# Layer 0 attention of a two-layer block: scores made once with queries on partitions, probabilities transposed on the array

## The reference

```python
h = _layernorm(x, axis=-1) * (1 + ca) + sa
q = (h @ Wq.T).reshape(B, S, 16, 64).transpose(0, 2, 1, 3)      # B = 2, S = 1024
k, v = ...                                                      # 4 heads each, repeated 4 times
scores = jnp.einsum('bhqd,bhkd->bhqk', q, k) * 64 ** -0.5
scores = scores + causal                                        # -inf above the diagonal
probs = jax.nn.softmax(scores, axis=-1)
out = jnp.einsum('bhqk,bhkd->bhqd', probs, v)
x = x + ga * (out.transpose(0, 2, 1, 3).reshape(B, S, 1024) @ Wo.T)
```

## Time and profile before

| | us |
|---|---|
| median of 3 runs | 1540.2 |
| lowest, highest | 1532.3, 1541.4 |
| span of the profiled execution | 1535.8 |
| layer 0 attention in it, first projection to last addition to y | 38.8 to 673.2 |
| one group of it in the steady part (215 to 525 us holds four) | 77.5 |

### The profile page before, as it was taken

How to read it: one execution, slowest core, us unless ns; L and a number is a source line. 1 busy time by engine, 2 the same in 40 slices (tenths; PEclk the granted TensorE clock), 3 DMA queues, 4 the chain that set the end, 5 groups by cost and what they waited for, 6 DMA issues and landing times. The chain is left out here.

```text
span 1535.8 us, 21410 instructions
## 1 busy us (share of the span) xinstructions
PE 1313.7 (86%) x7772; PEld 774.5 (50%) x7772; DVE 976.1 (64%) x1750; ACT 692.4 (45%) x1319; POOL 115.2 (7%) x155
## 2 busy tenths in 40 slices
PE   4688999999999999966999996526898888789998
PEld 3344444454545454444888874413343333256886
DVE  4455464545555454146999985756777666257998
ACT  2232334342424252433666665421566556525664
POOL 0000000000000000000000000120211111020000
PEclk9698999999999999987999998855899989868998
DMA  3101111120201020104576640022222210102220
GB/s 103 40 15 34 29 34 34 33 48 15 48 19 43 15 43 15 30 0 96 130 159 146 150 92 1 1 35 90 56 55 57 47 47 20 43 21 78 76 103 28
DMA packets 51476, 81.61 MB, mean 53 GB/s; under 512 B 16749, under 2 KB 34453, under 8 KB 47445
## 3 DMA queue, kind: packets, MB, share of 16 engines
q1 hardware_dynamic: 51004, 79.40, 21.1%
q10 hardware_dynamic: 384, 1.05, 0.6%
HBM read 63.75 MB, written 5.68 MB: 45 GB/s over the span
## 5 line engine op out<-in xcount | busy, mean ns | idle before, releaser
L621 DVE TENSOR_REDUCE mraw<-ps 128x1 f32<-128x512 f32 (+3 forms) x304 | 192.7, 659 | 131.1 <-PE ps L507 74.0
L1329 PE MATMUL ps<-qA 128*128 128x512 f32 x960 | 252.9, 400 | 15.2 <-POOL qA L1439 10.6
L723 ACT ACTIVATE shared<-ps 128x512 f32<-128x512 f32 (+1 forms) x216 | 119.4, 567 | 263.3 <-PE ps L540 261.9
L1046 DVE TENSOR_REDUCE mraw<-ps 128x2 f32<-128x1024 f32 (+3 forms) x160 | 173.7, 1114 | 67.6 <-PE ps L954 46.1
L1329 PEld LDWEIGHTS ps<-qA 128*128 128x128 f32 x960 | 182.1, 192 | 64.2 <-POOL qA L1439 12.3
L1101 ACT ACTIVATE shared<-ps 128x512 f32<-128x512 f32 (+2 forms) x320 | 154.4, 561 | 124.7 <-PE ps L970 124.4
L539 PE MATMUL ps<-qA,kH 128*128 128x512 f32 (+3 forms) x384 | 167.8, 447 | 5.8 <-DMA qB<-mT 5.8
L501 PE MATMUL ps<-kH,qA 128*128 128x512 f32 (+3 forms) x384 | 138.8, 415 | 34.9 <-DVE qA L611 18.8
L1393 ACT CAST qA<-shared 128x512 fp32r<-128x512 f32 x160 | 99.3, 621 | 90.4 <-DVE shared L1531 88.9
L1341 PE MATMUL ps<-qA,kH 128*128 128x512 f32 x480 | 136.3, 393 | 4.1 <-DVE qA L1455 4.1
L540 PE MATMUL ps<-qB,kL 65*128 65x512 f32 (+3 forms) x384 | 132.8, 356 | 0.0
(11 more groups left out here) (247 smaller groups left out, 1747.1 us busy)
## 6 DMA issues: line engine op xcount, KB each, us to landing
shared<-comb SPq DMA_DIRECT2D x92, 256.0 KB, 4.3
qB<-qA SPq DMA_DIRECT2D x16, 512.0 KB, 4.8
rB<-a0rec_dram SPq DMA_DIRECT2D x60, 128.0 KB, 2.9
shared<-comb SPq DMA_DIRECT2D x7, 1024.0 KB, 4.4
rB<-a1rec_dram SPq DMA_DIRECT2D x28, 128.0 KB, 2.6
e0wUp<-in_w SPq DMA_DIRECT2D x48, 64.0 KB, 4.6
qA<-q_split SPq DMA_DIRECT2D x24, 128.0 KB
q_split<-qA SPq DMA_DIRECT2D x4, 512.0 KB
```

What stands on the lines that cost most here:

```text
L621: nc.vector.tensor_reduce(out[:, h0:h0 + n_h, qt % 4], src, AX, ALU.max).then_inc(w_free, 1)
L723: nc.scalar.activation(probs(n)[:, hs[0]:hs[-1] + 1, lo:512], src, ACT.Exp, scale=scale)\
L1046: nc.vector.tensor_reduce(out[:, :, js[0]:js[-1] + 1, qt % 4], src, AX, ALU.max).then_inc(x_free, 1)
L1329: ins = nc.tensor.matmul(bank[0:M, :], w[par][:, at:at + M], h[:, cols], start=(r == 0), stop=(r == 2))
```

## The change

The attention of layer 0 is written anew; the other stages stay as they are.

- Scores are made once, with queries on partitions. A row m is one tile of 128 queries (qt) of one group, against its qt + 1 blocks of keys; the tiles are taken in the order 3, 4, 2, 5, 1, 6, 0, 7. A row is cut into units: all four heads at once for qt 0 and 1, two heads for 2 and 3, one head for 4 to 7. That is 22 units to a group.
- For each head and PSUM bank there is a "high" matmul (128 rows) and a "low" one (64 rows, `qA[0:64]` against `kL[0:64]`), and a mask matmul on the diagonal.
- `high` and `low` scale the queries by -0.125, so scores are negative. DVE takes the least of each row of a unit (`least_of`), ACT the exponential with that as bias and with the row's sum as a second result (`exps`), one instruction to a head.
- The probabilities are turned back, 128 x 128 at a time, by transposes on the array (`turn`): 144 to a group, four to a PSUM bank. ACT and DVE copy the banks out (`copy_turned`), 4 of 7 by ACT.
- Values are float32 matmuls with 64 columns of V as weights, two heads of 128 queries moving, two such side by side (columns 0 to 63 and 64 to 127 of the array). There are no matmuls with ones.
- One over the sums (`recip`, DVE, 128 x 4) is widened by POOL, turned by two transposes (`spread_rows`), copied by ACT, and multiplied in by DVE (`normalise`).
- The DMAs of the copy of q, of the maxima, of the sums and of their inverses are gone, with the triangle on POOL. `qB` and `rB` serve as room for turned probabilities; the constant `sel64` and the ones row of `kL` are gone.
- Projections, `fin` and turned probabilities share two banks (4 and 5), in the order of one plan; the scores have two slots of two banks, so unit s waits for the exponentials of unit s - 2.

```diff
-            (k.sel64[:, :, :], a["sel64"]), (k.dec[:, :], a["dec"]), (k.rope[:, :, :, :], a["rope"]),
+            (k.dec[:, :], a["dec"]), (k.rope[:, :, :, :], a["rope"]),
...
+    ORDER = (3, 4, 2, 5, 1, 6, 0, 7)
+    U = 1 + REP // 2
     LAG = 2
+    SLOTS = 2
+    P_RING = 4
+    PT_RING = 3
+    def heads_of(qt):
+        size = REP if qt < 2 else 2 if qt < 4 else 1
         return [tuple(range(h, h + size)) for h in range(0, REP, size)]
...
+    ROWS_OF = [(g, qt) for g in range(G) for qt in ORDER]
+    UNITS = [(m, hs) for m, (g, qt) in enumerate(ROWS_OF) for hs in heads_of(qt)]
+    NU, NM = len(UNITS), len(ROWS_OF)
...
+    def planned():
+        out = [("proj", 0, 0, j) for j in range(U)]
+        products = []
+        ready_jobs = {}
+        for g in range(G):
+            for i, (qc, j) in enumerate([(qc, j) for qc in range(2) for j in range(U)]):
+                if g:
+                    ready_jobs.setdefault(PER_GROUP * (g - 1) + 3 + 3 * i, []).append(("proj", g, qc, j))
+                elif qc:
+                    ready_jobs.setdefault(0, []).append(("proj", g, qc, j))
...
+            for m in [m for m in range(NM) if final_unit[m] + LAG == s]:
+                out.append(("recip", m))
+            blocks = []
+            for m in range(NM):
+                if first_unit[m] + LAG <= s <= final_unit[m] + LAG:
+                    blocks += [(m, b) for b in range(ROWS_OF[m][1] + 1) if closing_unit(m, b) + LAG == s]
+            credit = min(credit + 1.75, 3.0) if s < NU else 99.0
+            while products and products[0][-1] <= s and \
+                    (credit >= 1 or any(m - PT_RING >= products[0][1] for m, b in blocks)):
+                item = products.pop(0)
+                out.append(item[:-1])
+                credit -= 1
+                m = item[1]
...
+            turns = [("t", m, b, i) for m, b in blocks for i in range(4)]
+            out += woven(matmuls_of(s) if s < NU else [], turns)
+            for m in [m for m in range(NM) if final_unit[m] + LAG == s]:
+                out.append(("spread", m))
+                products += [("values", m, kt, s + 2) for kt in range(ROWS_OF[m][1] + 1)]
+            if s < NU:
+                out.append(("unit", s))
+            s += 1
+        return out
...
+                def score(e):
+                    kind, u, at, what, h = e
+                    m, hs = UNITS[u]
+                    g, qt = ROWS_OF[m]
+                    par = g % 2
+                    heads, lo, hi = banks_of(qt, hs)[at]
+                    opens = at == 0 and what == "high" and h == heads[0]
+                    if opens:
+                        if u == first_unit[m]:
+                            pe.wait_ge(dve_free, dve_taken[item["proj", g, qt // 4, U - 1] + 1])
+                        if u >= SLOTS:
+                            pe.wait_ge(p_done, u - SLOTS + 1)
+                    width = hi - lo
+                    bank = slot(u, at)
+                    if what == "mask":
+                        ends = bank[:, 0:len(heads) * width].rearrange("p (h w) -> p h w", w=width)[:, :, width - P:width]
+                        return nc.tensor.matmul(ends, k.ident_bf[:, :], k.masks[:, 1:2, :].broadcast_to((P, len(heads), P)),
+                                                start=False, stop=True, skip_group_check=True)
+                    i = heads.index(h)
+                    rows = slice(0, P) if what == "high" else slice(0, hd)
+                    keys = k.kH[par] if what == "high" else k.kL[par]
+                    return nc.tensor.matmul(bank[:, i * width:(i + 1) * width], k.qA[par][rows, h, qt * P:(qt + 1) * P],
+                                            keys[rows, lo:hi], start=(what == "high" and i == 0),
+                                            stop=(what == "low" and hi < (qt + 1) * P), skip_group_check=True)
+                def turn(e):
+                    kind, m, b, i = e
+                    x = item[kind, m, b]
+                    keys = ROWS_OF[m][1] + 1
+                    if i == 0:
+                        bank_free(x)
+                        pe.wait_ge(p_done, closing_unit(m, b) + 1)
+                    h, kt = divmod(4 * b + i, keys)
+                    u = unit_of_head(m, h)
+                    at = (h - UNITS[u][1][0]) * keys + kt
+                    ins = nc.tensor.transpose(work(x)[:, i * P:(i + 1) * P], probs(u)[:, at * P:(at + 1) * P],
+                                              k.ident[:, :])
+                    if i == 3:
                         ins.then_inc(w_full, 1)
+                def spread_rows(m):
+                    pe.wait_ge(widened, m + 1)
+                    if m >= 2:
+                        pe.wait_ge(on_done, m - 1)
+                    for p in range(2):
+                        ins = nc.tensor.transpose(out_bank(m)[:, 256 + p * P:256 + (p + 1) * P],
+                                                  wide(m)[:, p * P:(p + 1) * P], k.ident[:, :])
+                    ins.then_inc(spread_full, 1)
+                def values(m, kt):
+                    g, qt = ROWS_OF[m]
                     kv, b = divmod(g, B)
+                    if kt == 0:
+                        upto = item["t", m, qt] + 1
+                        pe.wait_ge(act_free, act_taken[upto])
+                        pe.wait_ge(dve_free, dve_taken[upto])
+                        pe.wait_ge(spread_done, m + 1)
+                    probs_t = turned(m)[:, 0:REP * (qt + 1) * P].rearrange("p (h t q) -> p h t q", h=REP, t=qt + 1)
+                    for i in range(2):
+                        ins = nc.tensor.matmul(out_bank(m)[hd * i:hd * (i + 1), 0:2 * P],
+                                               k.V[:, b * TPB + kt, kv * hd:(kv + 1) * hd], probs_t[:, i::2, kt, :],
+                                               start=(kt == 0), stop=(kt == qt), skip_group_check=True)
+                    if kt == qt:
+                        ins.then_inc(pv_done, 1)
...
+                def low(e):
+                    x = item[e]
+                    kind, g, qc, j = e
+                    par = g % 2
+                    cols = slice(qc * 512, (qc + 1) * 512)
+                    dve.wait_ge(q_hi, highs[x + 1])
+                    if j == 0:
+                        ins = nc.vector.tensor_tensor(k.kL[par][0:hd, cols], work(x)[0:hd, :],
+                                                      k.kH[par][0:hd, cols].bitcast(F32), ALU.subtract)
                     else:
+                        for i in range(2):
+                            h = 2 * (j - 1) + i
+                            ins = nc.vector.scalar_tensor_tensor(out=k.qA[par][hd:2 * hd, h, cols],
+                                                                 in0=work(x)[i * hd:(i + 1) * hd, :], scalar=-scale,
+                                                                 in1=k.qA[par][0:hd, h, cols].bitcast(F32),
+                                                                 op0=ALU.mult, op1=ALU.subtract)
+                    ins.then_inc(dve_free, 1)
...
+                def least_of(u):
+                    m, hs = UNITS[u]
+                    keys = (ROWS_OF[m][1] + 1) * P
+                    dve.wait_ge(s_full, u + 1)
+                    both = k.ps[:, 1024 * (u % SLOTS):1024 * (u % SLOTS) + 1024]
+                    if len(hs) == 2:
+                        src = both.rearrange("p (h w) -> p h w", h=2)[:, :, 0:keys]
                     else:
+                        src = both[:, 0:len(hs) * keys].rearrange("p (h w) -> p h w", w=keys)
+                    nc.vector.tensor_reduce(least(u)[:, 0:len(hs)], src, AX, ALU.min).then_inc(m_done, 1)
+                def copy_turned(m, b):
+                    x = item["t", m, b]
+                    dve.wait_ge(w_full, x + 1)
+                    if m >= PT_RING:
+                        dve.wait_ge(pv_done, m - PT_RING + 1)
+                    nc.vector.tensor_copy(turned(m)[:, 512 * b:512 * (b + 1)], work(x)).then_inc(dve_free, 1)
+                def recip(m):
+                    dve.wait_ge(p_done, final_unit[m] + 1)
+                    if m >= PT_RING:
+                        dve.wait_ge(widened, m - PT_RING + 1)
+                    nc.vector.reciprocal(recs(m), sums(m)).then_inc(rec_done, 1)
+                def normalise(m):
+                    g, qt = ROWS_OF[m]
+                    dve.wait_ge(pv_done, m + 1)
+                    dve.wait_ge(spread_done, m + 1)
                     if g:
+                        dve.wait_ge(w_full, item["fin", g - 1, qt // 4, 0] + 1)
+                    nc.vector.tensor_tensor(k.oN64[:, :, qt * P:(qt + 1) * P],
+                                            out_bank(m)[:, 0:2 * P].rearrange("p (a q) -> p a q", a=2),
+                                            spread(m).rearrange("p (a q) -> p a q", a=2), ALU.mult).then_inc(on_done, 1)
...
+                def exps(u):
+                    m, hs = UNITS[u]
+                    keys = (ROWS_OF[m][1] + 1) * P
```

(74 more changed lines are left out.)

493 lines of the change are left out of this document (136 added, 357 removed).

## The result

| | before | after |
|---|---|---|
| median, us | 1540.2 | 1618.7 |
| lowest, highest | 1532.3, 1541.4 | 1615.8, 1624.3 |
| span of the profiled execution | 1535.8 | 1616.6 |
| layer 0 attention, first projection to last addition to y | 38.8 to 673.2 = 634.4 | 39.5 to 753.4 = 713.9 |
| one group, steady | 74.3 | 88.0 |

The ratio is 1.0539, interval 1.0483 to 1.0596: slower. Of the 80.8 us between the two spans, 79.5 lie in the stage that was changed. What follows it takes 863.2 us after and 862.6 before.

The account below looks back on a forecast made before the run. PE bounds the kernel: 83.2 us a group against 63.7 before. 8 x 83.2 = 666, waits 38, start 7, end 6 make the stage 717 against 634.4, +82, so 1622 us; range 1565 to 1695.

Parts of the forecast that it names:

- The mechanism: PE score matmuls: when rows go from 128 to fewer or back, the next weight load waits until streaming ends, 0.09 to 0.11 us.
- The first rival: Low score matmuls: row changes cost nothing, PE 65.9 us and waits 9 a group, 1509 us; decides from about 0.07; chance 0.12.
- The price of a change: Around each low score matmul: 0.21 us going in and 0.15 coming out, about 0.18 per change of rows.
- The number of changes: Score matmuls of a group: 48 changes into low matmuls and 48 out, 17.3 us together.
- Transposes: PE transposes of probabilities and inverses: 144 + 16 a group at about 0.10 us on average, 16.0 us, all new.
- The rival that they run at the half clock: PE transposes at 1.2 GHz, 141 us more, 1763; chance 0.05 together with the array halves running in turn.
- Values: Values matmuls: 36 pairs a group at 0.43 us with both array halves at once, 15.5 us.
- The 31 us at the high end of the bounds: Values matmuls, per group, if the two halves of the array run one after the other; 1746 us in total.
- Visits to 64 columns: PE's switches to the values matmuls and back: 18.4 a group at 0.36 us both ways, 6.6 us.
- ACT and DVE: Softmax engines: ACT 52 us and DVE 48 us of work a group, neither reaching PE's 83.
- The rivals on waits and clock: Round trip binds: waits 13.8 a group, 1694, chance 0.15 (milder: 9, 1655); clock 5% less: 1657, chance 0.10.
- the account of the kernel before: Layer 0 attention before: group 77.5 us, set by PE, 63.7 of work and 13.8 of waits, mainly for job banks.

Follow-up runs that it names:

- e4_before_64_rows: The kernel before with its low score matmul cut from 65 rows to 64, leaving the maxima out of the scores: 1647.9 us, ratio 1.0724 to before.
- e1_low_128_rows: The changed kernel with the low score matmuls on all 128 rows, the 64 added rows of low keys being zero: 1512.0 us, ratio 0.9848 to before.
- e3_lows_side_by_side: The changed kernel, 64 rows kept, each unit's high matmuls first, then all low ones with no transposes between: 1557.2 us, ratio 1.0138 to before.
- e8_no_row_sums: e1_low_128_rows with the exponentials' row sums left out and rows divided by one: 1497.7 us, ratio 0.9754 to before.
- e5_proj_moved: e1_low_128_rows with the projections issued between steps 4, 6, 8, 12, 15, 19 instead of 3, 6, 9, 12, 15, 18: 1494.9 us, ratio 0.9728 to before.
- e6_values_longer_runs: e1_low_128_rows with values matmuls gathered into fewer, longer runs (8.9 visits per group in place of 18.4): 1532.3 us, ratio 0.9952 to before.
- e7_both: e1_low_128_rows with the edits of e5_proj_moved and e6_values_longer_runs together: 1499.7 us, ratio 0.9751 to before.

## Why the prediction was right, and where its working was not

The forecast was 1622 and the median is 1618.7; the stage was put at 717 and took 713.9. Point by point:

- **The mechanism** is the one named: the load that doesn't start under the running matmul when the rows go to 64 or back. It was read from two places in other stages and one at the values. The gap of 0.09 to 0.11 came back as 0.09 and 0.10. One kernel shows it without the change (e4_before_64_rows), one has the change but not the loss (e1_low_128_rows). The first rival, "a change of rows costs nothing", falls with 768 changes at 0.135 to 0.17 each, well over its point of 0.07.
- **The price of a change** was taken as 0.18, 0.36 for the pair. A low matmul compared with itself gives 0.34 for the pair, 0.17 each; PE's own work gives 0.17 (e1_low_128_rows) and 0.18 (e3_lows_side_by_side). The stage gives 0.135 to 0.148, because other waits grow when the changes are gone. The forecast for a low matmul with both changes, 0.6 us from start to start, came out as 0.51: 0.62 from transpose to transpose less the transpose's own 0.11. The missing part lies behind the next transpose, as its open load.
- **The number of changes**, 48 in and 48 out, was exact: 768 in 8 groups.
- **If the price is gone**: the first rival worked out 1509 for that case, with 65.9 of work and 9 of waits a group. e1_low_128_rows, where the price is taken away by other means, gave 1512.0 with 69.8 and 5.1: the same 74.9 for the group.
- **Transposes** came at 0.11 back to back, at the full clock. The rival that they run at the half clock falls: the clock was 0.98 with 144 of them in each group. By the Trainium skill, TensorE: Matmul & The Clock Gate, Part 4: PE-mode transpose, it shouldn't engage for them; the trace of after disagrees, at least for transposes woven between matmuls. **Values** ran with both halves of the array at once:

```profile
746.46 3.67 PE L608 MATMUL ps<-qB,shared 128*64 128x256 f32 x32
```

  32 records, 8 blocks of keys, 0.43 to a block and the latency of the last. The 31 us at the high end of the bounds are excluded.
- **Visits to 64 columns** were taken at 0.36 and cost 0.35. In after, 1.56 us pass from the transpose ahead of a visit of two blocks to the transpose behind the 512-column score that follows (median of 31). Without a visit between they are 0.35 apart (62 such), and two blocks are 0.86; 0.35 is left. Projections and `fin` stand at two records of 0.43 each, as forecast.
- **ACT and DVE** are busy 45.0 and 43.9 us in a group, where 52 and 48 were added up. ACT's records add to 51.2 and overlap by about 0.1 us at each joint, which the sum missed; the same holds for the read of a sum, taken at 0.208 and worth 0.09 (e8_no_row_sums). Copies and exponentials had the expected durations (585 and 1117 ns). Neither engine is near 88.
- **The rivals on waits and clock**: waits of PE were 1.9 us a group where 5.5 were forecast, far from 9 or 13.8; the clock stayed at 0.98, so the fall of 5% didn't come.

**What was wrong: the account of the kernel before.** The prediction took 215 to 525 us for four whole groups and so had 77.5 us to a group, 63.7 of them work and 13.8 a remainder that it called waits. The group is 74.3, so the remainder is 10.6. It seemed confirmed by adding three rows, but two of those, 19.6 and 16.0, are the load's and the matmul's view of one pause, as the pair of rows in e5_proj_moved showed. PE's records show only 3.4 us of idle time in a group. That isn't all of its waits either. In the trace of before:

```profile
299.71 0.19 PEld L501 LDWEIGHTS ps<-kH,qA 128*128 128x128 f32 x1 [0.29 <-DVE mraw L621]
```

```profile
299.71 0.50 PE L501 MATMUL ps<-kH,qA 128*128 128x512 f32 x1
300.04 0.34 PE L539 MATMUL ps<-qA,kH 128*128 128x384 f32 x1
300.22 0.33 PE L540 MATMUL ps<-qB,kL 65*128 65x384 f32 x1
```

The load waited for DVE to read a job bank and starts together with its matmul, which therefore takes 0.33 to the next, not 0.23: 0.11 of it is the open load. The matmul ahead (L540, 384 columns, start 299.40) had streamed by 299.6, so the array stood for some 0.2 us, and PE's records show none of it. In five groups 54 of the 512-column matmuls of L501 are like this. PE's own row for these waits shows little of them:

```profile
PE ps L501 <- DVE mraw L621: 10.7, 34, 0.8
```

An estimate from the starts, with 0.21 us of streaming to 512 columns and 0.11 to a load, puts 5 us of a group ahead of loads that L621 released and 2 ahead of those that L611 did. So the cause that the prediction named, job banks not yet read, is real and about half the size it was given; how the rest of the 10.6 divides was not settled.

**What was luck.** The forecast of the stage is a sum over the kernel after and doesn't use the group of before, so this error did not enter it. Within that sum three terms were off and cancelled. Per group, waits were 1.9 instead of 5.5 and the changes of rows 16.3 (48 x 0.34) instead of 17.3. Scores and transposes, by what is left of 88.0, were 37.5 instead of 33.6. The others (values 15.5, visits 6.6, projections and `fin` 8.6, masks 1.6) held within 0.2 each, and the total came to 88.0 for 88.7. The difference to before comes about otherwise than the prediction has it. It put +19.5 of work and -8.3 of waits to a group. The group grew by 13.7, with PE's idle time down by 1.5, and start and end of the stage shrank by 30 us: 8 x 13.7 - 30 is the 79.5. The prediction is right for the right reason about what decides, with a wrong account of the group it started from.

## What to carry to other kernels

Count, along the order in which PE gets its matmuls, how often one with at most 64 contraction rows (or output columns) stands beside one with more; each border costs about 0.17 us of PE's time here, of which 0.12 to 0.15 are seen in the stage. For rows, padding the operand with one row of zeros removes it for the price of a memset. Don't add wait rows: a load's wait and its matmul's are one pause. And don't take PE's idle time for all of its waits: a load that starts late is open, under a record that still counts as busy. Count the groups in a stretch by instructions, not by eye. Work that needs nothing new from the other engines is filler, and gathering it into long runs to save borders can cost more than it saves: e6_values_longer_runs lost 20 us that way (and 3 us in e7_both, with the projections moved), whereas moving six projections (e5_proj_moved) gained 17 and gives the fastest kernel here, 1494.9, 2.7% under before.

## What the runs showed of the hardware that was not expected

- The border lies between 64 and 65 rows. 768 changes between 65 and 128 rows cost nothing that can be told from none (1519.5 against 1512.0, intervals overlapping), 768 between 64 and 128 cost 104 us in the stage.
- The exposed part is the gap and the load: 0.34 us for the pair of changes, of which the two gaps are 0.09 and 0.10.
- A change of columns, into and out of matmuls with 64 output columns, costs 0.35 us for both ways, the same as a pair of row changes.
- The read of a sum behind an exponential has a record of 0.20 us but holds up ACT for only 0.09: without it, exponentials of 256 columns start 0.36 us apart instead of 0.45.
- A transpose right behind a 512-column score matmul seems to cost little: in e1_low_128_rows the low matmul starts 0.03 us after the transpose's start (631.54 and 631.57), and the 0.33 before it is the high matmul with the transpose's load. The pair of 0.35 is what counts. How the 0.33 divides was not tried.
- What follows the stage is the same code in all kernels and took from 852 to 867 us in the profiled executions, without order in what was changed ahead of it. Differences under about 1% between kernels are therefore read from the stage here, not from the total.
